# The last two layers of a four-layer cross-attention kernel, from eight token tiles in step to two token halves

## The reference, cut to what matters

```python
# layer 2 (index 2), its last part                        # B, S, D = 4, 256, 256
h = layer_norm(x, ln_mlp_scale, ln_mlp_offset)
x = x + gelu(h @ w_fc1 + b_fc1, exact) @ w_fc2 + b_fc2    # w_fc1 (256, 1024), w_fc2 (1024, 256)
# layer 3
h = layer_norm(x, ln1_w, ln1_b)
q = (h @ q_w + q_b)  -> 16 heads of 16                    # k, v from the context, 64 keys
attn = softmax(where(mask, q @ k.T / 4, -3.4e38))         # every token by itself over 64 keys
x = x + (attn @ v) @ cproj_w + cproj_b
h = layer_norm(x, ln2_w, ln2_b)
x = x + gelu(h @ fc_w + fc_b, tanh) @ proj_w + proj_b
```

## Time and profile before

| | |
|---|---|
| median of three runs | 795.4 us |
| profiled execution: span | 794.8 us |
| TensorE busy, of the span | 697.0 us, 88% |
| VectorE, ScalarE, GpSimd busy | 62%, 40%, 40% |
| mean granted TensorE clock | 0.940 |
| TensorE at the first product of feed-forward 1 | 622 us |
| first product of feed-forward 2 | 742 us |
| last `down` product ends | 792.3 us |

### The profile page before, as it was taken

The page is one execution under the profiler, slowest core; times in us unless marked ns, Lnnn a source line. Parts: engine busy times, 40 slices in busy tenths (PEclk is TensorE's granted clock), DMA queues, the critical chain, the costliest instruction groups (busy, mean ns, idle before and its releaser), DMA issues.

```text
span 794.8 us, 11731 instructions
## 1 busy us (share of the span) xinstructions
PE 697.0 (88%) x4432; PEld 509.8 (64%) x4432; DVE 492.8 (62%) x840; ACT 319.8 (40%) x693; POOL 318.4 (40%) x292
## 2 busy tenths in 40 slices
PE   6769989778978897699999999999998998795798
PEld 5446655447864454487757777875767897254588
DVE  4356677656555999546457674334797766498553
ACT  2044444423204777455532225652332411486311
POOL 4023444521524888453126640002675522286200
PEclk9578998999989999899999999999999999998899
DMA  5866742010006000004530000440000002000000
GB/s 174 226 161 187 215 116 46 2 35 0 1 1 211 1 1 1 2 22 163 188 106 1 1 1 19 148 152 1 0 1 1 1 1 92 15 1 1 0 27 27
DMA packets 40528, 46.70 MB, mean 59 GB/s; under 512 B 5697, under 2 KB 34970, under 8 KB 40346
## 3 DMA queue, kind: packets, MB, share of 16 engines
q1 hardware_dynamic: 38888, 44.46, 18.6%
q10 hardware_dynamic: 1586, 1.51, 0.7%
HBM read 37.72 MB, written 8.13 MB: 58 GB/s over the span
## 4 chain that ended last, share of the span: by engine, by line
PE 61%; DVE 20%; DMA 5%; ACT 4%; POOL 4%; issue 3%; ACTq 1%; SPq 1%; DVEq 0%; POOLq 0%
PE narrow_ps L510 8%; PE wide_ps L852 7%; PE wide_ps L491 6%; PE narrow_ps L887 5%; PE wide_ps L803 5%; PE wide_ps L839 3%; PE wide_ps L826 3%; PE wide_ps L543 3%; PE narrow_ps L693 3%; DVE scoresb L1376 3%; DVE mx L1385 2%; DMA wstream<-in_wqT 2%; PE wide_ps L471 2%; DVE sums L1392 2%; POOL probs L1684 2%
## 5 line engine op out<-in xcount | busy, mean ns | idle before, releaser
L1675 POOL TENSOR_TENSOR scoresb<-scoresb,mx 128x768 f32<-128x768 f32 (+1 forms) x40 | 70.7, 1769 | 152.5 <-DVE mx L1383 114.5
L1661 POOL TENSOR_TENSOR rstd<-veps,mhalf 128x1 f32<-128x1 f32 x56 | 33.2, 593 | 146.6 <-DVE veps L1304 146.6
L1051 ACT ACTIVATE probsT<-wide_ps 128x1024 f32<-128x1024 f32 x40 | 41.0, 1025 | 103.1 <-PE wide_ps L543 103.1
L1684 POOL TENSOR_TENSOR probs<-scoresb,rcp 128x1024 f32<-128x1024 f32 x40 | 78.2, 1955 | 7.0 <-DVE rcp L1393 7.0
L510 PE MATMUL narrow_ps<-wstream_r,hidden 128*128 128x256 f32 x576 | 71.9, 285 | 8.0 <-DVE hidden L1361 7.7
L510 PEld LDWEIGHTS narrow_ps<-wstream_r,hidden 128*128 128x128 f32 x576 | 70.8, 191 | 9.5 <-DVE hidden L1361 8.2
L491 PE MATMUL wide_ps<-xq_r,wstream_r 128*128 128x512 f32 x192 | 64.7, 419 | 4.8 <-issue 4.5
L543 PEld LDWEIGHTS wide_ps<-ident,probs 128*128 128x128 f32 x320 | 38.0, 146 | 46.5 <-issue 45.9
L543 PE MATMUL wide_ps<-ident,probs 128*128 128x128 f32 x320 | 44.3, 284 | 25.1 <-POOL probs L1684 23.3
L1444 DVE TENSOR_REDUCE mx<-wide_ps 128x2 f32<-128x640 f32 x64 | 49.6, 818 | 18.6 <-PE wide_ps L629 18.1
L803 PE MATMUL wide_ps<-scoresb_r,probs_r 128*128 128x256 f32 x256 | 55.7, 300 | 6.1 <-DVE vwb L1550 4.2
(11 more groups left out here) (182 smaller groups left out, 1526.3 us busy)
## 6 DMA issues: line engine op xcount, KB each, us to landing
wstream<-in_L_xattn_wk SPq DMA_DIRECT2D x8, 512.0 KB, 3.9
wstream<-in_L_xattn_wv SPq DMA_DIRECT2D x8, 512.0 KB, 5.1
wstream<-in_L_xattn_wo SPq DMA_DIRECT2D x8, 512.0 KB, 6.2
wstream<-in_wqT SPq DMA_DIRECT2D x8, 512.0 KB, 7.7
qrow<-qscratch SPq DMA_DIRECT2D x16, 192.0 KB
kscratch<-kparts SPq DMA_DIRECT2D x7, 320.0 KB, 2.4
qscratch<-qparts SPq DMA_DIRECT2D x8, 256.0 KB, 2.9
wstream<-in_L_xattn_mlp_w SPq DMA_DIRECT2D x2, 1024.0 KB, 5.3
```

The lines of the kernel that those rows point to most:

```text
L1051: nc.scalar.activation(dst, src, ACT.Identity, **kw).then_inc(ring.drained[ring.slot(key)], 1)
L1675: g.tensor_tensor(s3[:, first:], s3[:, first:], mx[:, u % 3, first:].unsqueeze(2).broadcast_to([P, 16 - first, n_scores]), ALU.subtract).t ...
L1684: g.tensor_tensor(probs[:, u % 2, :].rearrange("p (h k) -> p h k", h=16), s3[:, :, 0:T], rcp[:, u % 3, :].unsqueeze(2).broadcast_to([P, 16 ...
```

## The change

Layers before stay as they are, except that feed-forward 0 keeps its gelu result in a buffer of its own (`gelu`) and no longer in `scoresb`. The loop over steps and the common `mlp` are replaced, from 622 us on, by one written list for each of TensorE, ScalarE, VectorE and GpSimd. Half 0 now goes through `queries3`, scores, softmax, projection and into feed-forward 2 while half 1 is in `down` of feed-forward 1. TensorE's new list:

```diff
-            mlp(1, 4)
-            norm_turn(5)
-            queries(3, w3[0], ("ln", 5))
-            for step in range(-3, NQ + 2):
-                scores3(step + 3) ... turn_probs(step) ... values3(step - 1) ... project(4, step - 2)
-            mlp(2, 6)
+            up(1, 0, 0)  up(1, 0, 1)  norm_turn(4, (1,))  up(1, 0, 2)  up(1, 0, 3)  up(1, 1, 0)
+            down(1, 0)   down(1, 2)
+            up(1, 1, 1)  up(1, 1, 2)  norm_turn(5, (0,))  up(1, 1, 3)
+            queries3(0)  scores3(0)  scores3(1)
+            down(1, 4)
+            scores3(2)   turn_probs3(0)  scores3(3)  turn_probs3(1)  values3(0)
+            down(1, 6)
+            project3(0)  turn_probs3(2)  values3(1)  project3(1)  turn_probs3(3)  values3(2)
+            norm_turn(5, (1,))  project3(2)  values3(3)
+            queries3(1)  project3(3)  scores3(4)  scores3(5)
+            norm_turn(6, (0,))  scores3(6)
+            up(2, 0, 0)  up(2, 0, 1)  up(2, 0, 2)  up(2, 0, 3)
+            turn_probs3(4)  turn_probs3(5)  values3(4)  scores3(7)
+            down(2, 0)
+            project3(4)  values3(5)  turn_probs3(6)  project3(5)  values3(6)  turn_probs3(7)
+            project3(6)  values3(7)
+            down(2, 2)
+            project3(7)
+            norm_turn(6, (1,))
+            up(2, 1, 0) ... up(2, 1, 3)
+            down(2, 4)   down(2, 6)
```

Other edits:

```diff
-            act.wait_ge(prob_ready, probcount[...])      # at the head of mlp on ScalarE
+        gelu = sb("gelu", [P, 3, 1024])                  # gelu results no longer in scoresb
+        qT3 = xq[:, 2064:4112]...                        # queries of layer 3 beside x's high part
-            turn_probs: among=TURNS      scores3: among=SCORES
+            turn_probs3, scores3: any of the three wide slots
+            queries3(half): one wide slot per half, two copies of 512 columns each
-            sp.wait_ge(*narrow.full(("down", 1, NQ - 1)))
+            sp.wait_ge(*narrow.full(("proj", 3, NQ - 1)))   # fc_w of layer 3 into a buffer of its own
             sp.dma_start(*halves(mlp_load(2, 0), t["L3_xattn_fc_w"])).then_inc(load["mlp3_up"], 16)
+            sp.wait_ge(*wide.full(("up", 1, 1, 3)))
             sp.dma_start(*halves(mlp_load(2, 1), t["L3_xattn_proj_w"])).then_inc(load["mlp3_down"], 16)
-            weights_low(2, chunk) on VectorE, four times
+            weights_low2(chunk) on GpSimd, four times
+    nc = bacc.Bacc(..., dynamic_dma_scratch_size=256)
```

More of the change, by code:

```diff
@@ L473, in queries @@
                     m.then_inc(filled, 1)
-            PARTS = ((0, 0), (1, 0), (0, 1))
[L477 to L513, removed]
@@ new lines, in up @@
+            def up(n, half, fp, func, b1):
+                key = ("up", n, half, fp)
+                i = 8 * n + 4 * half + fp
+                act.wait_ge(*wide.full(key))
+                if i >= 3:
+                    act.wait_ge(hidden_split, i - 2)
+                for j in range(2):
+                    f = 2 * fp + j
+                    nc.scalar.activation(gelu[:, i % 3, j * 512:(j + 1) * 512],
+                                         wide_ps[:, wide.slot(key), j * 512:(j + 1) * 512], func,
+                                         bias=column(b1, f)).then_inc(wide.drained[wide.slot(key)], 1)
@@ L1081, in mlp, with mlp0 @@
+            def mlp0(between):
                 for half in range(2):
                     for fp in range(NF // 2):
[L1083 to L1092 removed]
@@ L1098, in mlp @@
+                        if half == 1 and fp == 0:
                             between()
@@ L1282, in _, with attended3, turned3, exp3 @@
-            mlp(2, ACT.Gelu_apprx_tanh, "L3_fc_b", (6, "L3_ln2_w", "L3_ln2_b"))
+            def attended3(q):
+                key = ("ao", 3, q)
+                act.wait_ge(*narrow.full(key))
+                for c in range(NC):
+                    evac(qT3[:, c, qoff(q)], narrow_ps[:, narrow.slot(key), c * P:(c + 1) * P], narrow, key,
+                         bias=column("L3_v_b", c))
+            def turned3(q):
+                probs_turned(base["3"] + q)
+            def exp3(q):
+                exp(base["3"] + q, 1024)
@@ new lines, in _ @@
+            weights_high2(0)
+            up1(0, 3)
+            weights_high2(1)
+            up1(1, 0)
+            up1(1, 1)
+            up1(1, 2)
+            norm_turned(5, "L3_ln1_w", "L3_ln1_b", (0,))
+            up1(1, 3)
+            queries3(0)
+            exp3(0)
+            exp3(1)
+            exp3(2)
+            turned3(0)
+            turned3(1)
+            attended3(0)
+            exp3(3)
+            weights_high2(2)
+            turned3(2)
+            attended3(1)
+            weights_high2(3)
@@ L1285, in _ @@
+            attended3(6)
+            turned3(7)
+            attended3(7)
+            norm_turned(6, "L3_ln2_w", "L3_ln2_b", (1,))
+            for fp in range(NF // 2):
+                up2(1, fp)
         @block.vector
@@ L1638, in _ @@
+            for fp in range(NF // 2):
+                hidden_parts(2, 1, fp)
+            for q in range(NQ // 2, NQ):
+                down2(q)
         @block.gpsimd
```

470 lines of the change are left out of this document (348 added, 122 removed).

## The result

The kernel became slower: 803.9 us (median of 801.8, 803.3, 803.9, 804.2 and 804.3) against 795.4 us for the kernel before on the same chip, a ratio of 1.008 with a 95% interval of 1.0042 to 1.0117. Some executions are slower as a whole (four of 25 of the kernel before, in the sets of the later experiments, took 801.7 to 807.9 us); the ratios leave those out and are not the quotient of the two medians (here 1.011, inside the interval). The forecast was 792.6 us, the range 785 to 800.

A forecast was written before the change was run, and what follows sets the result against it. TensorE was taken as the bound: 136.6 us of work from 622 on, 33.7 of waits and half clock to win from. The walk's 793.2, or 790.7 without contention, gave 792.0, plus 0.6: 792.6 us, range 785 to 800.

The forecast's parts named there:

- walk: Sum along the new lists with old durations, from 622 us on; it claimed a span of 793.2 us, chance 0.48.
- X: Time 694.2 us, when project3(1) gets the slot of project3(0); later events are counted from it.
- hole A: Before turn_probs3(1): TensorE waits 3.5 us for normalize(1), behind shift(2) on GpSimd.
- hole B: Before the second projection: project3(1) waits 2.6 us for the residual of project3(0) on VectorE.
- hole C: Before feed-forward 2's first product: 3.0 us waiting for x_parts, as ScalarE has exp(4) ahead of the turned copy.
- hole D: Before turn_probs3(7): 4.7 us, as GpSimd has two rstd and two rows ahead of normalize(7).
- hole E: Before up(2,1,0): 4.5 us, waiting for the chain from projection 7's residual to the cast.
- Step 1: Up to 648.7 us: nothing lost; two new weight splits may slow two casts by 1.4 us each, needed 3 us later.
- Steps 2 to 4: From 648.7 us to feed-forward 2's first products: holes of 3.5, 2.6 and 3.0 us, with 1.3 for low clock.
- Step 5: Early feed-forward 2: normalize(4) and a split precede shift(6), exps delay the gelu to X+31.2; up(2,0,3) ends X+34.0.
- two contention terms: 1.1 us before the second projection and 1.4 before the last probability transposes; without them the span is 790.7.
- The slower one: Between down(1,4) and turn_probs3(7), GpSimd and VectorE block one another: five hits of 1.15 to 1.37, 800 us; chance 0.19.

The follow-up runs named there:

- splits back: Kernel after with all four weight splits of feed-forward 2 moved from GpSimd to VectorE; ratio to the kernel before 0.9996.
- hole B mended: Kernel after with middle3(3) and normalize3(3) before down1(6), and project3(0)'s residual before two normalizations; ratio to the kernel before 1.0055.
- hole D mended: Kernel after with normalize3(7) directly behind shift3(7) on GpSimd, ahead of two rstd and two rows; ratio to the kernel before 0.993.
- six edits: Kernel after with four splits on VectorE, list entries moved for holes A, B, D, E and a ScalarE copy before exp(4) for hole C; 783.47 us, ratio 0.9789.

## Why the prediction was wrong, point by point

The walk named a place and a size for each event, so it can be held against the trace. Times from the start of the stretch; the walk's are its own less 627.58 (for the last two X = 694.2, and 779.3).

| from | to | walk | after | difference |
|---|---|---|---|---|
| start | `up(1,1,1)` starts | 21.1 | 24.7 | +3.5 |
| there | hole A ends | 31.7 | 31.7 | 0.0 |
| there | `down(1,6)` ends | 8.6 | 10.0 | +1.4 |
| there | hole B ends (X) | 5.2 | 5.7 | +0.5 |
| X | hole C ends | 19.9 | 21.7 | +1.8 |
| there | hole D ends | 34.6 | 35.5 | +0.9 |
| there | hole E ends | 16.3 | 17.2 | +0.9 |
| there | last `down` products | 14.3 | 13.5 | -0.8 |

- **Step 1, "up to 648.7, nothing", is the step that failed.** It was 3.5 us, the largest term (2.2 in the second profile of the kernel after, again the largest). Its own sentence had the right instructions and the wrong size: "slow two casts by 1.4 us each", taken from 2.06 - 0.69, "but the products that need them come 3 us later". 1.4 was about what remained of a GpSimd instruction when that cast began (629.13 - 627.61 = 1.52), not the price of a meeting. Here the meetings cost 2.91 - 0.69 = 2.2 and 3.28 - 1.23 = 2.05, together 4.3, on one chain; the cover was about 2 (in the kernel before this part was ready at 636.5, and the 12 products ahead of its own end at about 638.7). The hole is 2.12 in both profiles; low clock behind it was 1.3 in one and nothing in the other. The experiment with the splits back has 20.95 for this part.
- The second meeting was of a kind that I had left out: I counted casts and normalizations, and it was a subtraction. Both ended just behind a split (635.86 and 639.17, behind 635.30 and 638.08). I had taken my price, 1.4, from one slowed row; the two meetings cost 2.2 us beside a split of 3.18 and 2.05 beside one of 2.64, some 0.7 and 0.8 of the other's instruction.
- **Holes A, B, C, D and E were right**: 3.5, 2.6, 3.0, 4.7 and 4.5 forecast, 3.69, 3.13, 3.43, 5.12 and 2.19 + 2.36 measured, at the named instructions, and for all but C, where the profile names none, with the named releasers. In the single experiments moving a list entry changed just the hole at which it was aimed, but only D went whole: 2.69 of A came back one product later, 1.15 of B and the 2.36 of E stayed.
- **Steps 2 to 4, the low clock, were mis-sized.** I allowed 1.3 us behind A and nothing behind B. Behind A transposes, values and `down(1,6)` took 10.0 us where 7.3 were work: 2.7 lost, and 1.6 in three other profiles with the same hole. Behind B the transposes took 1.91 and the values 0.89 where the earlier trace rows have 1.00 and 0.57 to the next row: most of the 1.8 to hole C (with hole B mended it went down by 1.5). Behind D, where I had allowed 2.1, it was 755.08 to 759.67, 4.6 us for 2.6 of work, 2.0. The term behind D was about right and that behind A near the cheap end; I had put none where the old trace's hole of 2.98 had cost only 0.4.
- **Step 5, the late gelu, was right**, the fourth split ahead of shift(6) included. The exps push the gelu back (forecast X+31.2 less 1.3, X+29.9; measured 729.98, X+32.1, late by little more than the 1.8 that hole C's end was late). After the table load the gelu starts at once:

```profile
728.69 1.28 ACT L1160 ACT_TABLE_LOAD   x1
729.98 3.58 ACT L1160 ACTIVATE gelu<-wide_ps,col 128x512 f32<-128x512 f32 x6
```

So going by the row, 747.84 + 1.28 and the gelu at 749.14, was right here: the load took 1.28 us and the gelu began 0.01 us behind it.
- **Two terms of the walk stood without a row**, a handover of 0.1 to 0.2 us and a `norm_turn` of a half of about 0.9. In the trace of before a handover took 0.08 us from VectorE to GpSimd (reciprocal ends 705.02, `normalize` starts 705.10) and 0.12 from GpSimd to TensorE (703.02 to 703.14); in the kernel after the eight transposes start their successor after 0.79 us (625.97 to 626.76). Neither made the miss.
- **From the walk to 803.9.** The walk's span was 793.2. The stretch added 8.1 (6.7 by the second profile) and began 1.6 earlier, which gives the 799.9 of the profile, but for 0.2. To that come 1.9 from span to time in that execution and 2.1 from that execution to the median. I had made it +0.6 from my profile's span to the median; the times of the executions that list both lie about 2 us above their spans, so the profile of before was most likely that of its slowest run (796.77) and not of one near the median. And 1.2 I had taken off when I halved two contention terms. 8.1 - 1.6 + 0.2 + 1.9 + 2.1 - 0.6 + 1.2 = 11.3, the whole miss. The profiled execution was the fastest of the five, so 2.1 us of the miss lie in no row here.
- **The rivals.** The slower one had the right mechanism with the wrong place and size: between `down(1,4)` and `turn_probs3(7)`, five hits of 1.2 us. The decisive pair of hits lay earlier and was larger. Its price of 800 us was nearest to the result, in part by luck, since it came from five meetings and one pair decided. It does not explain all: with the splits back the holes of the order are left, and they make the difference between a ratio of 0.9996 and one of 0.9789. The sign that I gave for the slow side did not show: from the end of `scores3(2)` to the transposes behind hole A it took 6.4 us, forecast 6.2, and 6.5 was the limit named.

What is shown: the hole in `down(1,0)` comes from the first two splits; all of D, the first part of E, 2.0 us of B and 1.0 us of A each from an entry in a list, with the low clock behind D and B; 1.6 us between C and D from the fourth split; that the same products behind the same hole take longer at a lower granted clock (0.71 in the first 2.7 us behind 639.23, 1.00 at the same place in the second profile). What stays open: why in one execution the clock falls behind a hole of 2 to 4 us and in another not, and what would take the rest of hole C and of hole E out.

## What to carry to other kernels

Where instructions of two engines stretch one another, as VectorE's cast (0.69 to 2.91 us) and subtraction (1.23 to 3.28) did here beside GpSimd's splits of 3.18 and 2.64, price a meeting by the length of the other's instruction, not by one slowed row, and ask which result of the slowed engine is due next. Where a hand-written order makes a hole, look for the one list entry that stands ahead of the releaser (`normalize3(7)` behind four short instructions cost some 6 us), and move it only after walking the list behind it. A hole on TensorE cost up to twice its length here: 4.6 us less idle time than the mean of the kernel after brought 6.2 us with hole D mended, and 11.0 brought 20.7 with six edits. And compare profiles place by place: the sum over a stretch mixes an edit with the luck of the clock elsewhere.

## What the runs showed of the hardware that I had not expected

- A subtraction of VectorE (`hidden` from `gelu` and `hidden`) was stretched from 1.23 to 3.28 us beside a GpSimd split, as much as a cast (0.69 to 2.91), and the splits themselves from 2.40 elsewhere in the trace to 3.18 and 2.64. In the four meetings read here VectorE's instruction ended behind the other's by a distance that repeats: 0.54 and 0.56 for two casts, 1.08 and 1.09 for two subtractions.
- The same hole, with the same code on either side, is followed by low clock in one execution and by full clock in another: after the 2.12 us in `down(1,0)` 84 products took 11.56 or 10.24 us, after 3.7 us the eight transposes 1.94 or 1.06, after 2.7 us 48 products 7.45 or 5.92.
- The stretch began between 623.4 and 634.5 us in the profiles of kernels whose code up to there is the same: 11 us, more than the effect under study. Ratios of timed runs carry the verdicts here, and the stretch tells where the time went.
